# The tokenizer's last sixteen heads go from SBUF to their rows of h, one transfer a head

## What is computed

```python
# H, N, L = 128 heads, 64 states, 512 positions; W = x: 16 sequences
P = dt_Lambda[..., None] * t            # heads x states x positions
S = jnp.exp(P - P_max[..., None])
Wc = Wc * num * recip
K = jnp.einsum('chn,hnl->chl', Wc, S).real       # 16 x 128 x 512
h = jnp.concatenate([cls_tok, K], axis=1)        # 16 x 129 x 512
h = h + attn(layernorm(h)); h = h + ffn(layernorm(h)); ...
```

## Time and profile before

| | |
|---|---|
| time, median of 3 runs | 1567.52 us (1565.58 to 1571.8) |
| profiled execution, its own time | 1569.5 us |
| its span, first to last instruction | 1567.7 us |
| PE busy | 1390.0 us, 89% of the span |
| DVE, POOL, ACT busy | 836.6, 480.3, 378.3 us |
| tokenizer's last product to scan's first transpose, PE idle | 17.6 us |
| chain at that place: last store, load, statistics | 5.09, 5.63, 2.48 us |

### The profile page before, as it was taken

One profiled execution on the slowest core, in us unless ns is written; L12 is line 12 of the kernel. 1 busy time (PEld: TensorE's weight loads), 2 busy tenths in 40 slices (PEclk: granted clock), 3 DMA queues, 4 the chain that ended last, 5 costly groups with the idle time before them and its releaser, 6 DMA issues.

```text
span 1567.7 us, 21991 instructions
## 1 busy us (share of the span) xinstructions
PE 1390.0 (89%) x6461; PEld 1079.8 (69%) x6462; DVE 836.6 (53%) x1728; ACT 378.3 (24%) x736; POOL 480.3 (31%) x350
## 2 busy tenths in 40 slices
PE   0686639999999999389999889999999999999997
PEld 0584317888544444237776578888888889999896
DVE  8975597655322222573667775555555543333332
ACT  3114114121111111242223312233333212222221
POOL 0752330252244443100211025532332203243332
PEclk9999779999999999689999999999999999999999
DMA  4591005202865554600000503656666569776443
GB/s 100 110 155 20 0 22 182 101 21 81 307 133 93 92 88 72 202 22 0 1 0 1 182 21 109 207 195 215 213 215 225 198 257 361 247 198 187 77 74 41
DMA packets 88403, 197.04 MB, mean 126 GB/s; under 512 B 28256, under 2 KB 32224, under 8 KB 84832
## 3 DMA queue, kind: packets, MB, share of 16 engines
q1 hardware_dynamic: 68240, 154.20, 30.4%
q0 software_dynamic: 20096, 42.02, 14.6%
HBM read 112.24 MB, written 81.02 MB: 123 GB/s over the span
## 4 chain that ended last, share of the span: by engine, by line
PE 79%; DVE 12%; issue 3%; DMA 2%; ACT 2%; POOLq 1%; POOL 0%; DVEq 0%; ACTq 0%; SPq 0%
PE ps L1546 25%; PE ps L1606 19%; PE ps L1668 9%; PE ps L2073 6%; PE ps L1694 4%; PE ps L442 4%; PE ps L1636 2%; PE ps L551 2%; DVE held L495 2%; PE ps L1682 1%; PE ps L791 1%; PE ps L2042 1%; PE ps L792 1%; PE ps L2098 1%; DVE held L1313 1%
## 5 line engine op out<-in xcount | busy, mean ns | idle before, releaser
L1606 PE MATMUL ps<-moe_rounded 128*128 128x384 f32 (+2 forms) x1800 | 374.7, 350 | 0.0
L1606 PEld LDWEIGHTS ps<-moe_rounded 128*128 128x128 f32 x1800 | 326.3, 188 | 33.2
L1313 DVE SCALAR_TENSOR_TENSOR held<-ps,moe_scratch,held 128x512 f32<-128x512 f32 (+1 forms) x255 | 187.6, 747 | 180.9 <-PE ps L1546 179.9
L1546 PE MATMUL ps<-moe_expert_parts,moe_rows_parts 128*128 (+1 forms) x1320 | 258.2, 348 | 2.6 <-DVE moe_rows_parts L1337 1.5
L1546 PE MATMUL ps<-moe_rounded 128*128 128x512 f32 (+3 forms) x885 | 242.3, 394 | 11.8 <-DVE moe_rounded L1295 9.8
L1546 PEld LDWEIGHTS ps<-moe_expert_parts,moe_rows_parts 128*128 128x128 f32 (+1 forms) x1320 | 219.5, 190 | 15.7 <-issue 3.3
L1546 PEld LDWEIGHTS ps<-moe_rounded 128*128 128x128 f32 (+2 forms) x885 | 146.8, 171 | 50.7 <-DVE moe_rounded L1295 12.0
L1323 DVE TENSOR_TENSOR moe_scratch<-moe_scratch,ps 128x256 f32<-128x256 f32 (+1 forms) x80 | 37.7, 471 | 237.2 <-ACT moe_scratch L1528 237.2
L1668 PE MATMUL ps<-moe_experts,moe_scratch 128*128 x320 | 144.2, 593 | 0.6 <-issue 0.6
L1417 POOL TENSOR_TENSOR moe_split_parts<-moe_scratch,moe_split_parts 128x704 fp32r<-128x704 f32 (+2 forms) x48 | 88.7, 1853 | 172.9 <-ACT moe_split_parts L1510 172.8
L1401 POOL DMA_INDIRECT slot_tokens<-moe_scratch x68 | 73.5, 1081 | 174.2 <-DVE held L1313 167.5
(11 more groups left out here) (312 smaller groups left out, 1689.0 us busy)
## 6 DMA issues: line engine op xcount, KB each, us to landing
moe_expert_parts<-expert_parts SPq DMA_DIRECT2D x8, 3840.0 KB, 13.0
expert_parts<-moe_split_parts SPq DMA_DIRECT2D x32, 704.0 KB
moe_scratch<-in_ffn_gate_up SPq DMA_DIRECT2D x32, 352.0 KB, 5.0
xn_rows<-moe_xn SPq DMA_DIRECT2D x2, 4096.0 KB, 12.9
moe_experts<-in_ffn_gate_up SPq DMA_DIRECT2D x8, 1024.0 KB, 6.3
expert_parts<-moe_split_parts SPq DMA_DIRECT2D x8, 1024.0 KB
moe_scratch<-in_ffn_sh_gate_up SPq DMA_DIRECT2D x15, 512.0 KB, 3.5
tokens<-sb SPq DMA_DIRECT2D x16, 256.0 KB
```

The lines of the kernel that those rows point to most:

```text
L1313: v.scalar_tensor_tensor(out=hb[0:rows, t, :], in0=ps[0:rows, ADDED[t % 3], :], scalar=sg[0:rows, t:t + 1], in1=hb[0:rows, t, :], op0=ALU. ...
L1546: mm = t.matmul(out, lhs(k, x), rhs(k, y), start=(k == 0 and i == 0), stop=(k == ks - 1 and i == 2))
L1606: mm = t.matmul(unit_banks(u, m)[j], weights(k, x, j), xT[y][:, k, unit_cols(m)], start=(k == 0 and i == 0), stop=(k == KD - 1 and i == 2))
```

## The change

Chunks 0 to 6 are stored and loaded as before, though the load of chunk 5 now stands ahead of both halves of chunk 7. Chunk 7 is neither stored nor loaded. In its place `straight(k, b)` waits for the half's `evac` and issues eight transfers, one a head, from the 128 partitions of `ob` (256 bytes on each) to the head's partition of `hb` (128 runs of 256 bytes, one behind the other: 32 KB). All raise `h_in[0]`, so DVE waits for its new total, 16 x (7 + 16), and no more for `h_in[1]` to `h_in[3]`.

```diff
+        def straight(k, b):
+
+            sp.wait_ge(evac, 2 * k + b + 1)
+            for h in range(b * H8, (b + 1) * H8):
+                sp.dma_start(hb[k * HC + h:k * HC + h + 1, 0:NB, :].rearrange("h c (i j) -> h (c i) j", j=TJ),
+                             ob[:, k % 2, h * TJ:(h + 1) * TJ].unsqueeze(1)).then_inc(h_in[0], 16)
+
         last = NHC - 1
-        for k in range(NHC):
+        for k in range(last):
             store(k, 0)
...
+        load_chunk(last - 2)
+        straight(last, 0)
         load_chunk(last - 1)
-        sp.wait_ge(stored[last % 2], 16 * NHC)
-        heads = slice(last * HC, NH)
-        for g in range(NQ):
-            sp.dma_start(hb[heads, 4 * g:4 * g + 4, :], rows_of(heads, 4 * g, 4 * g + 4)).then_inc(h_in[g], 16)
+        straight(last, 1)
...
-                if t % NQ == 0:
+                if t % NQ == 0 and H_LOADED[t // NQ]:
                     v.wait_ge(h_in[t // NQ], H_LOADED[t // NQ])
...
-TOK_LOADED, TOK_STORED = (5 * 16, 6 * 16, 6 * 16), (6 * 16, NHC * 16, NHC * 16)
+TOK_LOADED, TOK_STORED = (5 * 16, 6 * 16, 6 * 16), (6 * 16, NHC * 16, (NHC - 2) * 16)
...
-H_LOADED = [16 * NHC, 16, 16, 16, 16]
+H_LOADED = [16 * (NHC - 1 + HC), 0, 0, 0, 16]
```

## The result

The changed kernel takes 1581.09 us (median of 4 runs, 1579.26 to 1582.37), the kernel before 1568.42 us in the same comparison (4 runs, 1565.58 to 1571.8): a ratio of 1.0081, with a 95% interval of 1.0066 to 1.0096. That is 12.7 us more, 10.3 to 15.1 by the interval. The profiled execution took 1581.69 us, with a span of 1579.9 us; the mean granted TensorE clock is 0.968, and was 0.965 before, so the clock was no lower and explains none of it.

A forecast was written before the change was run, and what follows sets the result against it. Bound: the start of DVE's first statistics, 122.67 us. Chunk 5's load to 113.0, two halves of 9.4 us around chunk 6's 3.7, plus 0.7, give 136.2: 13.5 later, 1567.5 + 13.5 = 1581.0 us; range 1571 to 1587.

The forecast's parts named there:

- What bounds: Tokenizer's end: the start of DVE's first statistics, 122.67 us, sets the stage's price; every microsecond there is one of the program.
- What is taken away: Tokenizer's end: chunk 7's two stores and the last round trip, store 5.09 us plus loads 5.63, 10.7 us of chain.
- What is moved: Chunk 5's load issued earlier, its packets from 109.3 to 113.0; chunk 6's load behind the first eight straight transfers.
- the sum: Packets in issue order: chunk 5's load to 113.0, first half 122.4, chunk 6's load 126.1, second half 135.5; DVE 136.2.
- door: Way into SBUF shared by four neighbouring partitions; all engines sending to one partition share its 25 to 37 GB/s, 28 taken.
- What is added: issue: SP's issue of the sixteen straight transfers: 0.43 to 0.65 us each, 3.4 to 5.2 us for eight.
- What is added: data: Straight transfers into one partition of h: 28 GB/s, 1.17 us for a head's 32 KB, 9.4 us a half.
- The rate follows the width of the destination: Transfers into SBUF: the number of destination partitions, whatever the source, limits the rate; 123 GB/s into sixteen, 430 into 128.
- Two doors at once: Rival for the straight transfers: two doors work side by side, blocks at 50 GB/s or more; chance 0.14.
- No door: Rival: one partition takes all sixteen engines send, 1.1 to 2.1 us a half, 1564.4 to 1567.3 us; chance 0.09.
- A worse door: Rival: 256-byte runs into one partition get 20 GB/s, 13.1 us a half, 20.9 us later, 1588.4 us; chance 0.09.
- One engine: Rival: one engine carries each whole head, 17.8 us a half, 30 us later in all, 1597.8 us; chance 0.04.

The follow-up runs named there:

- three chunks together: The kernel before, with chunks 5, 6 and 7 brought by the four last loads (48 partitions), through DRAM: 1563.49 us, ratio 0.9967.
- the wide run: The changed kernel, its sixteen transfers sent to 128 partitions of a free piece of SBUF instead of one partition of h: DVE starts at 122.90.
- the alternating order: The changed kernel with each half's heads issued in the order 0, 4, 1, 5, 2, 6, 3, 7: 1575.97 us, ratio 1.0044.

## Why the prediction was right

The forecast was 13.5 us more and 1581.0 us; 12.7 more and 1581.09 us were measured. That the two totals agree to 0.1 us is chance: the kernel before had a median of 1567.5 us when the forecast was made and of 1568.42 in the comparison. By the prediction's own steps:

*What bounds.* Right. The stage's end is DVE's start, and all that follows shifts with it: the first scan starts at 165.90 before and at 180.65 in the changed kernel (14.75 later, DVE's rows below), the statistics 14.76 later. From there to the end the shift shrinks to 12.2 us in the two profiled spans (1567.7, 1579.9); this is less than the 6.4 us by which these stages differed between two executions of one kernel, and no run here ties it to the change.

```profile
180.65 5.14 DVE L649 TENSOR_TENSOR_SCAN sb<-sb 64x2064 f32<-64x2064 f32 x1
```

*What is taken away.* Right in the trace: the store's and the load's 10.7 us are gone. But the later runs show that they were partly a price of standing behind chunk 5's and 6's loads: the same round trip costs 2.56 + 5.50 with three chunks together, and 5.39 + 3.34 with two.

*What is moved.* Chunk 5's load was to start at 109.3 and to be done at 113.0. In the packets of 108 to 112 us it starts from 108.5 on, one engine after another as each is done with the store, and not in one burst:

```profile
GB/s 85 90 105 154 156 504 476 182 837 504 187 504 169 1137 753 1357 18 18 18 18 18 335 0 0 0 0 0 0 0 0 0 0 0 0 0 0 0 13 13 10
```

So the first straight packets start before 112, a microsecond earlier than I had it. Chunk 6's load, 3.7 us in the sum, behaved otherwise than I thought: by the trace's packet records its sixteen 32 KB packets are under way for 6.4 to 8.4 us each (chunk 5's for 3.1 to 3.9), though they go to other partitions than the first half's. In the run onto 128 partitions, where no door holds the first half, the same load's packets take 3.2 to 4.3. So what stands behind a busy door's packets on the engines waits with them; the last ends at 127.2, where the sum had 126.1.

*What is added: issue.* Taken at 0.43 to 0.65 us each; 5.06 and 5.26 for eight are 0.63 and 0.66, at the upper end. It was rightly held to be off the path here. The run onto 128 partitions shows that it becomes most of the path as soon as the door is away: 122.90, and not the 119.6 to 122.5 of the rival without a door. That rival's sum has about 2 us from an issue to its packets, read from chunk 7's second store; this was a misreading. With three chunks together the same store is issued at 111.84 and its packets start at 112.7 or so; the 2 us were the engines, still at chunk 5's load.

*What is added: data.* The step on which all rested, and the mechanism was right: against the changed kernel two queues on two fours of partitions gain 6.9 us, two queues on one four 1.3, which is within the spread. Its size was off in the costly direction: a door at 28 GB/s, measured 25 in the saturated stretches, so a half is not 9.4 but 10.5 us. The second half's packets start at 125.0 and all has landed at 137.3. With 112.0 for the first half's start and 10.5 us for each half the prediction's own sum gives 112.0 + 10.5 + 3.7 + 10.5 + 0.7 = 137.4, and 137.43 came. The two errors, 1.0 us too late and 2.2 too short, cancel in part, which is luck; 136.2 was forecast. One thing isn't tested: packets of the constants run behind the second half's, between 128 and 137 us, and no run leaves them out, so whether they delay its end is not shown.

"The rate follows the width of the destination" was too simple a reading of the earlier trace rows. It holds from 16 to 32 partitions (131 to 203 GB/s) and not from 32 to 48 (154).

*The packets as I said they would look* (0.15 us each, a burst of sixteen 32 KB packets between the halves) weren't seen so. They take 0.18 us and more, and the 32 KB packets start one by one between 116.5 and 120.8, while other engines still send to the door; then nothing starts until 125.0.

*The rivals.* Two doors at once doesn't come by itself in order 0 to 7, but does with another order: 130.45 and 129.00, not the 126.8 I had for it. No door: refuted by 25 GB/s, and by the wide run, which is what it would have looked like. A worse door than 28 was the better guess within its direction, though 25 is nearer to the forecast than to its 20. One engine: its price was 17.8 us a half, and the second half had landed 12.3 us after its first packet. Packets filled 135.9% of sixteen engines' span, 22 open at a time; the trace doesn't name the engine of a packet, so that all sixteen shared them is inferred.

## What to carry to other kernels

Cutting a round trip through DRAM can pay only if the direct transfer's destination is wide: one that lands on one partition ran at 25 GB/s with the sixteen engines behind it, and what stood behind it on the engines waited along. Wide is not enough either: sixteen transfers onto 128 partitions had DVE start at 122.90, no earlier than the round trip did. Where such transfers can't be avoided, order them so that neighbours in time aren't neighbours in partition, and count their issue, 0.6 us each on one queue. Before shortening a chain of transfers, look at what else occupies the engines at its end: here the loads of chunks 5 and 6, which stood in the last store's and the last load's way, cost 2 to 2.6 us of the 10.7, and merging them into the last loads gained that much.

## What the hardware did that I had not expected

- Packets to a busy door start well before the door can take them: up to 103 GB/s, before the rate falls to 25. And in the second half the last 256-byte packets start some 4 us before DVE is let go. The start of a packet tells little of where its bytes are.
- The order of transfers on a single queue matters: 7.0 and 8.4 us between 0 to 7 and the alternating order in two executions, with no second queue. That the reserve of started packets is the reason is my reading, not shown.
- A 32 KB packet on one queue keeps its engine from the packets of another queue: the last store landed after 9.38 us on ACT's queue, with the loads of chunks 5 and 6 under way on SP's, and after 2.56 us when no load was under way.
- 48 partitions took loads more slowly than 32: 154 against 203 GB/s.
